# A four-layer graph network on one core: adjacency blocks of layer one begun at the end of layer zero and built six steps before they are applied

## What is computed

```python
def _L1_gnn_ref(H, edge_index, W):
    src, dst = (edge_index[0], edge_index[1])
    new_H = jax.ops.segment_sum(H[src], dst, num_segments=H.shape[0])
    return jax.nn.relu((H + new_H) @ W)

x = _layernorm(x + _L0_gnn_ref(x, src, dst, W_w, W_b, a_w, a_b), axis=-1)
x = _layernorm(x + _L1_gnn_ref(x, edge_index, L1_gnn_W), axis=-1)
x = _layernorm(x + _L2_gnn_ref(x, edge_index, edge_attr_4, ...), axis=-1)
x = _layernorm(x + _L3_gnn_ref(x, edge_index, edge_type_64, ...), axis=-1)
```

## Time and profile before

| | |
|---|---|
| median of 3 runs | 1089.12 us (1088.42 to 1090.14) |
| the profiled execution | 1089.84 us, its span 1088.0 us |
| PE busy | 1002.6 us, 92% of the span |
| DVE busy | 861.1 us, 79% |
| ACT busy | 691.3 us, 64% |
| POOL busy | 218.2 us, 20% |
| granted TensorE clock, mean | 0.971 |
| chain that ended last | PE 81%, DVE 10%, ACT 4%, issue 3%, DMA 2% |

### The profile page before, as it was taken

One profiled execution on the slowest core, in us unless ns is written; L12 is line 12 of the kernel. 1 busy time (PEld: TensorE's weight loads), 2 busy tenths in 40 slices (PEclk: granted clock), 3 DMA queues, 4 the chain that ended last, 5 costly groups with the idle time before them and its releaser, 6 DMA issues.

```text
span 1088.0 us, 27899 instructions
## 1 busy us (share of the span) xinstructions
PE 1002.6 (92%) x10463; PEld 874.7 (80%) x10463; DVE 861.1 (79%) x1934; ACT 691.3 (64%) x1489; POOL 218.2 (20%) x260
## 2 busy tenths in 40 slices
PE   3798979699999999995999999779999999989997
PEld 3343557599999999995788889669999999976775
DVE  6875999988998989987766677788787888766754
ACT  3467765454555555456888888577677776776554
POOL 4501340000000000000000000126666666610000
PEclk9899999899999999997999999889999999999998
DMA  6000020366767677752866564235444445334232
GB/s 159 1 2 1 4 68 3 121 207 225 238 215 225 222 238 227 204 175 72 292 195 193 172 201 141 82 104 140 138 136 129 131 131 139 109 112 124 69 99 82
DMA packets 86925, 150.38 MB, mean 138 GB/s; under 512 B 14524, under 2 KB 58375, under 8 KB 86557
## 3 DMA queue, kind: packets, MB, share of 16 engines
q1 hardware_dynamic: 65609, 116.01, 35.9%
q10 hardware_dynamic: 16122, 22.16, 5.7%
q0 software_dynamic: 5056, 10.36, 3.9%
HBM read 112.56 MB, written 35.94 MB: 136 GB/s over the span
## 4 chain that ended last, share of the span: by engine, by line
PE 81%; DVE 10%; ACT 4%; issue 3%; DMA 2%; POOL 0%; POOLq 0%; DVEq 0%; SPq 0%; ACTq 0%
PE PS L2500 14%; PE PS L2705 14%; PE PS L2488 11%; PE PS L2688 8%; PE PS L2611 7%; PE PS L2791 6%; PE PS L2581 3%; PE PS L2588 3%; PE PS L2326 2%; PE PS L2339 2%; DVE ring L1659 2%; DVE vo L1663 2%; PE PS L2403 2%; ACT X L1227 1%; PE PS L2357 1%
## 5 line engine op out<-in xcount | busy, mean ns | idle before, releaser
L1151 ACT CAST vo<-XT 128x768 f32<-128x768 bf16 (+1 forms) x218 | 180.3, 827 | 163.7 <-PE PS L2705 64.2
L984 POOL DMA_INDIRECT XT<-tab,ring x158 | 159.9, 1012 | 113.5 <-PE PS L2705 60.2
L2500 PE MATMUL PS<-vo 128*128 128x133 f32 x1300 | 175.9, 284 | 1.2 <-ACT vo L1151 1.2
L2500 PEld LDWEIGHTS PS<-vo 128*128 128x128 f32 x1300 | 157.2, 191 | 1.4 <-issue 1.4
L2488 PE MATMUL PS<-kp,ring 128*128 128x132 bf16 x1950 | 146.7, 221 | 3.2 <-DVE ring L1631 1.7
L2705 PE MATMUL PS<-vo 128*128 128x128 f32 x984 | 132.8, 279 | 0.0
L2488 PEld LDWEIGHTS PS<-kp,ring 128*128 128x128 bf16 x1950 | 125.6, 97 | 5.4 <-DVE ring L1631 1.8
L1641 DVE TENSOR_TENSOR XT<-iotab,XT 128x768 bf16<-128x768 bf16 (+1 forms) x218 | 120.0, 551 | 3.2 <-DMA hots_d<-XT 1.5
L2705 PEld LDWEIGHTS PS<-vo 128*128 128x128 f32 x984 | 118.9, 191 | 3.0 <-issue 2.4
L2490 PE MATMUL PS<-SDP,ring 128*128 128x12 bf16 x650 | 110.2, 170 | 0.0
L1286 ACT CAST adjf_r<-PS 128x512 fp32r<-128x512 f32 (+1 forms) x175 | 92.4, 550 | 25.4 <-PE PS L2581 23.6
(11 more groups left out here) (350 smaller groups left out, 2008.6 us busy)
## 6 DMA issues: line engine op xcount, KB each, us to landing
ring<-rows_d SPq DMA_DIRECT2D x146, 416.0 KB, 5.8
hots_d<-XT ACTq DMA_DIRECT2D x108, 192.0 KB, 4.7
big<-hots_d SPq DMA_DIRECT2D x10, 640.0 KB, 5.3
XT<-hots_d SPq DMA_DIRECT2D x10, 640.0 KB, 4.8
adj_d<-ring SPq DMA_DIRECT2D x20, 320.0 KB, 2.4
big<-hots_d SPq DMA_DIRECT2D x8, 480.0 KB, 4.4
adj_d<-ring SPq DMA_DIRECT2D x15, 240.0 KB, 2.1
ring<-adj_d SPq DMA_DIRECT2D x11, 320.0 KB, 3.0
```

The lines of the kernel that those rows point to most:

```text
L984: G.indirect_dma_start(far_rows[:, f % FBUF, :], None, tab[2], bass.IndirectOffsetOnAxis(ap=far_row[:, t:t + 1], axis=0)).then_inc(far_in[ ...
L1151: C.copy(ohd[:, k % 3, 0:n, :], ohb[:, k % 3, 0:n, :]).then_inc(hots_wide, 1)
L2500: T.matmul(bank(6 + b % 2)[:, 0:VW], ohd[:, k % 3, i, :], vals[:, k % 3, i, :], start=j == 0, stop=j == JN - 1).then_inc(scattered, 1)
```

## The change

- DVE's `set_hots` of the first group moves: the extra one and steps 0 to 5 are written inside layer zero, in batches 103 to 108, behind the weighted values of the batch. The copy on ACT that they need (of `SLc`) moves to batch 101.
- SP loads the first two chunks once the batches that they hold are stored (batches 0 to 17), not all. The loads of the third and fourth chunk stay behind `crow`; the wait for all stored batches is now there.
- PE's build 0 waits for the last values and the last sums of layer zero. The transpose of the counts goes behind build 3, into another bank.
- PE's order is now: builds 0 to 5, then for even s: build s + 6 and s + 7, apply s and s + 1.
- ACT makes the wide copies 0 to 3 ahead of the normalisation's root, and their byte copies behind it.
- DVE's byte copies run six steps behind `set_hots` in place of four. Some copies at group ends are taken a few steps later.
- XBUF (4), the four PSUM banks and the waits of a build and of a wide copy are as before.

```diff
+    EARLY_HOTS = HT * (NU - 1) // BT - 3
+    AHEAD = 6
@@ SP
             for r in range(3):
-                sp.wait_ge(hots_out[r], hots_stored(r))
+                sp.wait_ge(hots_out[r], 16 * len(range(r, (len(even(0)) * JN - 1) // BT + 1, 3)))
...
                 if n == 0:
                     sp.wait_ge(hots_wide, NBATCH)
+                    for r in range(3):
+                        sp.wait_ge(hots_out[r], hots_stored(r))
                     hots_load(2)
                     hots_load(3)
...
-                if c == 1 and q:
+                if c == 2 and q:
                     rel_store(q - 1)
@@ ACT
+                if k == EARLY_HOTS - 2:
+                    C.copy(SLc[:, 1, :, :], SLc[:, 0, :, :]).then_inc(pairs_ready, 1)
...
-            C.copy(SLc[:, 1, :, :], SLc[:, 0, :, :]).then_inc(pairs_ready, 1)
+            def block_wide(s):
+                w = even_width(s // NB)
+                act.wait_ge(adj_mm, s + 1)
+                if s >= XBUF:
+                    act.wait_ge(applied, s - XBUF + 1)
+                    dve_copied(act, s - XBUF)
+                C.copy(adjf[:, s % XBUF, 0:w], adj_bank(s)[:, 0:w]).then_inc(adjf_cp, 1)
+
+            def block_byte(s):
+                if not by_dve(s):
+                    adj_free(act, s)
+                    C.copy(adj_slot(s), adj_bank(s)[:, 0:even_width(s // NB)]).then_inc(adj_act, 1)
+
+            for s in range(XBUF):
+                block_wide(s)
             for h in range(2):
                 deviations(1, h)
+            for s in range(XBUF):
+                block_byte(s)
...
-            C.copy(crow[:, :], bank(7)[0:NB, 0:P]).then_inc(rc_cp, 1)
+            C.copy(crow[:, :], bank(4)[0:NB, 0:P]).then_inc(rc_cp, 1)
...
-                    act.wait_ge(adj_mm, s + 1)
                     if s >= XBUF:
-                        act.wait_ge(applied, s - XBUF + 1)
-                        dve_copied(act, s - XBUF)
-                    C.copy(adjf[:, s % XBUF, 0:w], adj_bank(s)[:, 0:w]).then_inc(adjf_cp, 1)
-                    if not by_dve(s):
-                        adj_free(act, s)
-                        C.copy(adj_slot(s), adj_bank(s)[:, 0:w]).then_inc(adj_act, 1)
+                        block_wide(s)
+                        block_byte(s)
...
-                    if q and b == 9:
+                    if q and b == 12:
                         rel_rows(q - 1)
@@ DVE
+                if k == EARLY_HOTS:
+                    dve.wait_ge(pairs_ready, 3)
+                    set_hots(0, NB, ohx[:, 0, :])
+                if 0 <= k - EARLY_HOTS < AHEAD:
+                    set_hots(0, k - EARLY_HOTS, ohs[:, k - EARLY_HOTS, :])
...
                     variance(1)
-                    set_hots(0, NB, ohx[:, 0, :])
                     scale(0)
...
-                    set_hots(q, b, ohs[:, s % SBUF, :])
-                    if s >= 4:
-                        adj_copy(s - 4)
+                    if s >= AHEAD:
+                        set_hots(q, b, ohs[:, s % SBUF, :])
+                    if s >= AHEAD:
+                        adj_copy(s - AHEAD)
                     if q == 0:
                         for i in range(BANKS):
-                            if b == min(1 + i, NB - 1):
+                            if b == (1 + i if i < HBANK - 1 else 2 * i + 2):
                                 dve.wait_ge(xp_top, i + 1)
...
-                    if q and b == 5:
+                    if q and b == 8:
                         sums_out1(q - 1)
@@ PE
-            pe.wait_ge(cnt_ready, 1)
-            T.transpose(bank(7)[0:NB, 0:P], rc[:, :], ident[:, :]).then_inc(rc_tr, 1)
...
-                if s == 3:
-                    pe.wait_ge(rc_cp, 1)
+                if s == 0:
+                    pe.wait_ge(vals_ready, NBATCH)
+                    pe.wait_ge(sums_cp, NB)
...
+                if b == 0 and q == 1:
+                    pe.wait_ge(rc_cp, 1)
...
-            build(0)
-            build(1)
+            for s in range(XBUF):
+                build(s)
+            pe.wait_ge(cnt_ready, 1)
+            T.transpose(bank(4)[0:NB, 0:P], rc[:, :], ident[:, :]).then_inc(rc_tr, 1)
+            for s in range(XBUF, AHEAD):
+                build(s)
             for s in range(0, NS, 2):
-                for n in (s + 2, s + 3):
+                for n in (s + AHEAD, s + AHEAD + 1):
                     if n < NS:
                         build(n)
```

More of the change, by code:

```diff
@@ L163, in up2_at @@
         return up_at(i) + 4
+    EARLY_HOTS = HT * (NU - 1) // BT - 3
+    AHEAD = 6
+    assert EARLY_HOTS + AHEAD - 1 < NBATCH
     LAST_ODD = max(k for k in range(NBATCH - 1) if k % 2 and k >= 3 and len(batch(k)) == BT)
@@ L1651, in _, with set_hots @@
             FIRST = [h for h in units_at(0) if HT * h < 2 * BT]
+            def set_hots(q, j, buf):
+                V.tensor_tensor(buf.rearrange("p (k n b) -> p k n b", k=3, b=4), IN1[:, :, :].rearrange("p (k n) b -> p k n b", k=3),
+                                SLc[:, :, j, 4 * q:4 * q + 4].unsqueeze(2).to_broadcast([P, 3, NREL, 4]), ALU.is_equal).then_inc(ohs_ready, 1)
             dve.wait_ge(pool_consts, 8)
@@ L1947, in split @@
                 low(BANKS - 1)
[L1949 to L1953, removed]
             normalise(1, X)
@@ L1975, in _ @@
                         dve.wait_ge(rel_mm, s - SBUF + 1)
-                    set_hots(q, b, ohs[:, s % SBUF, :])
-                    if s >= 4:
-                        adj_copy(s - 4)
+                    if s >= AHEAD:
+                        set_hots(q, b, ohs[:, s % SBUF, :])
+                    if s >= AHEAD:
+                        adj_copy(s - AHEAD)
                     if q == 0:
                         for i in range(BANKS):
-                            if b == min(1 + i, NB - 1):
+                            if b == (1 + i if i < HBANK - 1 else 2 * i + 2):
                                 dve.wait_ge(xp_top, i + 1)
                                 V.tensor_tensor(XL[:, nodes(i), :], X[:, nodes(i), :], XH[:, nodes(i), :].bitcast(fp32), ALU.subtract).then_inc(xp_rest, 1)
-                    if q and b == 5:
+                    if q and b == 8:
                         sums_out1(q - 1)
-            for s in range(BANKS * NB - 4, BANKS * NB):
+            for s in range(BANKS * NB - AHEAD, BANKS * NB):
                 adj_copy(s)
@@ L2525, in sums @@
                     pe.wait_ge(ag_ready, BANKS)
-                    pe.wait_ge(crelT_cp, BANKS)
+                    pe.wait_ge(crel_cp, BANKS)
                     pe.wait_ge(rc_cp, 1)
```

## The result

The changed kernel takes 1177.5 us (median of 4 runs, 1176.9 to 1179.9), against 1089.6 us before (4 runs, 1088.4 to 1091.1). The ratio is 1.081, with a 95% interval of 1.080 to 1.082: **slower by 88 us**. Forecast were 1170 us and a range of 1150 to 1197.

The account below looks back on a forecast made before the run. PE was taken to set the pace. Layer one's end was put at 758.6 against 680.9, +77.7 us, plus 2.5 for waits: +80.2 on 1089.1, rounded to 1170 us, range 1150 to 1197.

Parts of the forecast that it names:

- The ring: Layer one: eight unapplied blocks fill all places; PE and ACT wait for each other, 2.96 us a round against 1.95.
- The start: Layer one up to build 10: build 10 at 526.9 instead of 524.93 and four applications fewer, together 3.9 us lost.
- The byte copies: ACT's byte copies of steps 0 and 2 stand between the normalisation's root and rows: 2 x 0.48 us.
- DVE's slip: Extra set_hots in layer zero's batches 103 to 108 delay DVE's last instructions by 1.6 us, its variance by about 1.1.
- The stretch from build 10 on: Layer one, build 10 to last application: 133.2 + 90.0 + 2.5 + 6 = 231.7 us, against 156.0 before.
- 2.5 for waits: Semaphores before builds and wide copies, looked at after the wait, not during it: 0.03 us a round, 2.5 us.
- The rival of the clock: Pauses in each round of layer one sink the clock to the lower level: 1230 us; chance 0.07.
- The work between groups: Layer one's own rows, transposes and small copies between groups: between 0 and 11.5 us, 6 taken.
- the ring is hidden: Rival: ACT's wide copy can begin before its application is done, so only +3.9 us counts: 1093 us; chance 0.03.
- the kernel gets faster: Rival: PE's 10.0 idle us before the first build, less 2.1 us slip, are gained: 1081 us; chance 0.05.
- the change doesn't do what it says: Rival: first one-hots or builds still wait for a late layer-zero semaphore; 1165 to 1175 us, no separate chance given.
- The four applications lost before build 10: At build 10 PE has done applications 0 to 3 only, not 0 to 7: four of 0.48 us, 1.9 us.

## Why the prediction was right

ACT's wide copies of steps 20, 40, 50, 70 and 90 in the changed kernel, by which the stretch is measured below:

```profile
546.05 0.59 ACT L1269 CAST adjf_r<-PS 128x512 fp32r<-128x512 f32 x1 [1.37 <-PE PS L2602]
...
578.45 0.59 ACT L1269 CAST adjf_r<-PS 128x512 fp32r<-128x512 f32 x1 [1.36 <-PE PS L2602]
...
593.54 0.59 ACT L1269 CAST adjf_r<-PS 128x512 fp32r<-128x512 f32 x1 [1.10 <-PE PS L2602]
...
624.25 0.59 ACT L1269 CAST adjf_r<-PS 128x512 fp32r<-128x512 f32 x1 [1.36 <-PE PS L2602]
...
660.68 0.59 ACT L1269 CAST adjf_r<-PS 128x512 fp32r<-128x512 f32 x1 [1.36 <-PE PS L2602]
```

- **The ring was the term that decided, and its size held.** Rounds of 2.96 us on average were forecast. By ACT's wide copies of steps 40 and 50 (578.45 and 593.54) five rounds take 15.09 us, 3.02 each; by those of steps 150 and 160 (739.17 and 751.39) a 384-wide round takes 2.44, against 2.40. Taking out places (10, 9, 8) gave 1093, 1114 and 1177 us, and taking ACT's copies out of the ring 1134: the theory named each within its range, and no rival does. Only the slots were varied; that a PSUM bank counts like a slot is read from the waits in the code and fits the count of eight, but no run changed the banks.
- **The start.** Build 10 was put at 526.9 and came at 525.30; the rows of the normalisation, forecast 2.1 us late, came 0.54 late (506.83 against 506.29). The byte copies cost nearly what was forecast: DVE's first shift ends at 506.01, and the two copies (505.89 to 506.94) hold the rows back by 0.8 us, against 1.0. What was too large is DVE's slip. Its first variance came at 504.81 in place of 504.58. Layer zero ended 0.67 us earlier in this execution (499.10 against 499.77), which no term foresaw, so counted from there the slip is 0.9 us, not 1.6. The extra `set_hots` stood behind the variances, not ahead of them; with it gone the shift came 0.24 us earlier than before (506.01 against 506.25), 0.43 later when counted from layer zero's end, against 1.1.
- **The stretch from build 10 on was undersized by 9.5 us**: 231.7 and 2.5 for waits forecast, 243.7 measured. The overshoot of the start hid 1.6 of it, so the total came within 8 us by some luck. Four terms, estimated from ACT's wide copies. The average rounds, 0.06 and 0.04 us longer, make 4.2 us, where 2.5 had been put down for waits: 1.8 too few. The rival of the clock came true for a stretch: 0.50 from 635 to 645 us. The wide copies of steps 70 to 90 take from 624.25 to 660.68, 36.4 us; those of steps 20 to 40, with the same work between groups and clock 1.00, from 546.05 to 578.45, 32.4: some 4 us. The work between groups was given 6 of 11.5 us and comes out near 8; the round with a group's first build, for one, takes 550.74 - 547.26 = 3.48 us against 2.91. The last 2 us are at the two ends of the stretch, where the first builds still run at the lower clock (0.69 from 525 to 530 us).
- **The rivals.** That the ring is hidden, and that the kernel gets faster, are refuted by the waits above. That the change doesn't do what it says is refuted by the first build at 499.48. The clock rival priced a clock that stays low; from 530 us on it fell once, for some 15 us of 240, and cost about 4 in place of 57. The four applications lost before build 10 were real (PE had applied blocks 0 to 3), but with places enough the 1.9 us put down for them don't show: two, four and six steps ahead (six slots) took 1092.75, 1093.48 and 1093.41 us.

The Trainium skill, Perfetto Trace Analysis, Optimization Strategy, says that a gap that repeats on the engine that should be saturated can mean too few buffers for the next tile. The traces agree: 73 waits of 44.0 us in all on ACT's copies in the changed kernel, and none between 540 and 680 us with six slots.

## What to carry to other kernels

Count places before you raise a distance: blocks made and not used, against every buffer that they can lie in. Where the two were equal here, each side waited for the other's last step, and a round took the whole trip around (3.02 us for 1.95). One place to spare gave back 63 of 84 us, two gave all. And an early start is worth only what its next gate allows: here it needed a load moved ahead of an unrelated wait on the same queue.

## What the runs showed of the hardware

After 100 us at clock 1.00 the changed kernel's granted clock fell to 0.50, the lower of the two levels (1.2 GHz), in the windows from 635 to 645 us, and was back at 1.00 from 650 on. PE had worked in bursts, with waits of up to 0.8 us between them, all that time. In the variants with a shorter ring (five slots, or all byte copies on DVE) the clock stayed at 1.00 from 535 us to the end of layer one, and so it did with two steps ahead. The Trainium skill, TensorE: Matmul & The Clock Gate, A second HAM failure mode: psum-queue depth-cycling, describes a clock that swings under short idles; this trace agrees with it once in 240 us. Why it fell just there stays open: no run was made for it. The mean granted clocks of the four executions, 0.964 to 0.967, lie close together, and by an estimate from the windows the profiled one (0.966) would have had 0.972 without this fall, so the others probably had one of its size too.
